# Causal attention with an image token and a tanh recurrence: another beginning and end, image values in column groups, two heads' transposes together

## The reference

```python
q, k, v = split(x @ c_attn_w + c_attn_b)
k_img, v_img = cond @ uk_w.T + uk_b, cond @ uv_w.T + uv_b      # one key, one value a sequence
scores = q @ concat(k_img, k).T / sqrt(32);  scores = where(kj <= qi + 1, scores, -10000)
x = x + (softmax(scores) @ concat(v_img, v)) @ c_proj_w + c_proj_b
xw = x @ Wx + b
h = tanh(h @ Wh + xw[t])  for t in 0..511, h starts as cond;   out = x + h
```

## Time and profile before

| | |
|---|---|
| median of 3 runs | 1640.55 us |
| profiled execution, its span | 1643.75 us, 1642.0 us |
| TensorE busy | 1532.6 us (93%) |
| VectorE, ScalarE, GpSimd busy | 778.3, 665.1, 186.5 us |
| the chain that ended last | PE 86% of the span |
| TensorE's clock in 40 slices | 8 in the second and third, 9 in all others (tenths; 9 is 90% or more) |
| half clock inside the span | about 54 to 67, 81 to 85, 95 to 105 and 1505 to 1511 us, and after the last step |

### The profile page before, as it was taken

How to read it: one execution, slowest core, us unless ns; L and a number is a source line. 1 busy time by engine, 2 the same in 40 slices (tenths; PEclk the granted TensorE clock), 3 DMA queues, 4 the chain that set the end, 5 groups by cost and what they waited for, 6 DMA issues and landing times.

```text
span 1642.0 us, 74143 instructions
## 1 busy us (share of the span) xinstructions
PE 1532.6 (93%) x32749; PEld 1225.9 (75%) x32749; DVE 778.3 (47%) x2687; ACT 665.1 (41%) x2257; POOL 186.5 (11%) x300
## 2 busy tenths in 40 slices
PE   7799999999999999999999999999999999998775
PEld 6677887877777787877878778687787677777554
DVE  4455454445454545545455454554554454554221
ACT  3444444344343434344443443444534444443111
POOL 2111111010110101001010110100101011100000
PEclk9889999999999999999999999999999999999999
DMA  7323122212222223223332232333332332331000
GB/s 231 107 63 82 50 69 66 69 52 71 65 73 75 79 67 92 74 72 88 85 91 77 81 97 75 109 84 84 107 92 72 110 98 82 116 100 28 16 10 15
DMA packets 167903, 130.24 MB, mean 79 GB/s; under 512 B 54264, under 2 KB 153112, under 8 KB 167072
## 3 DMA queue, kind: packets, MB, share of 16 engines
q1 hardware_dynamic: 153792, 92.92, 19.9%
q0 software_dynamic: 13792, 32.58, 7.3%
HBM read 100.00 MB, written 25.43 MB: 76 GB/s over the span
## 4 chain that ended last, share of the span: by engine, by line
PE 86%; DVE 4%; issue 4%; ACT 4%; SPq 1%; DMA 1%; POOL 0%; DVEq 0%; POOLq 0%
PE rec L1056 27%; PE dense L986 10%; PE dense L502 9%; PE dense L504 7%; PE dense L503 7%; PE rec L1047 7%; PE scores L978 5%; PE pv L1003 4%; PE pv L1021 2%; PE scores L1056 2%; DVE pre L882 1%; PE dense L1063 1%; ACT probs L686 1%; ACT states L735 1%; PE dense L1014 1%
## 5 line engine op out<-in xcount | busy, mean ns | idle before, releaser
L1056 PE MATMUL rec<-wh,states 128*32 128x128 f32 x15360 | 516.3, 275 | 19.9 <-ACT states L735 19.2
L1056 PEld LDWEIGHTS rec<-wh,states 128*32 128x32 f32 x15360 | 399.3, 110 | 107.3 <-ACT states L735 46.1
L882 DVE STREAM_TRANSPOSE pre<-rec 128x128 f32<-128x128 f32 x480 | 152.0, 317 | 502.6 <-PE rec L1056 501.2
L735 ACT ACTIVATE states<-pre 128x32 f32<-128x32 f32 x512 | 133.9, 262 | 508.6 <-DVE pre L882 507.6
L686 ACT ACTIVATE probs<-probs,nmax 128x64 f32<-128x64 f32 (+7 forms) x512 | 271.3, 532 | 104.9 <-DVE nmax L826 102.5
L826 DVE CUSTOM_DVE_ANT_0 probs<-scores,msk,nimg 128x64 f32<-128x64 f32 (+7 forms) x512 | 245.2, 502 | 14.6 <-PE scores L978 6.4
L986 PE MATMUL dense<-ident,probs 128*128 128x128 f32 (+1 forms) x1254 | 229.2, 288 | 19.0 <-DVE probsT L836 7.0
L986 PEld LDWEIGHTS dense<-ident,probs 128*128 128x128 f32 (+1 forms) x1254 | 129.2, 135 | 82.1 <-issue 56.7
L502 PE MATMUL dense<-xT_hi,wqkv_hi 128*128 128x256 f32 x488 | 149.6, 307 | 6.7 <-DVE nimg L812 3.5
L836 DVE COPY probsT<-dense 128x256 f32<-128x256 f32 (+4 forms) x240 | 120.2, 501 | 63.3 <-PE dense L986 57.9
L694 ACT COPY probsT<-dense 128x256 f32<-128x256 f32 (+4 forms) x246 | 104.3, 424 | 107.0 <-PE dense L986 106.5
(11 more groups left out here) (138 smaller groups left out, 1766.3 us busy)
## 6 DMA issues: line engine op xcount, KB each, us to landing
vbuf<-v_dram SPq DMA_DIRECT2D x64, 192.0 KB, 2.7
xin<-x SPq DMA_DIRECT2D x64, 128.0 KB, 2.6
v_dram<-vbuf POOLq DMA_DIRECT2D x64, 128.0 KB, 2.8
out<-outs POOLq DMA_DIRECT2D x32, 256.0 KB, 4.2
vbuf<-v_dram SPq DMA_DIRECT2D x64, 128.0 KB, 2.4
kt<-k_dram SPq DMA_DIRECT2D x16, 512.0 KB, 5.6
vbuf<-v_dram SPq DMA_DIRECT2D x32, 256.0 KB, 3.2
k_dram<-knew POOLq DMA_DIRECT2D x60, 128.0 KB, 2.7
```

The costliest lines, as they stand in the source:

```text
L735: act.activation(state_cells(g), pre[:].rearrange("p f (b z) -> p f b z", z=GROUP)[:, :, :, s], ACT.Tanh).then_inc(h_ready, 1)
L882: dve.transpose(pre_all, rec_bank(g // GROUP)[:, 0:P]).then_inc(pre_ready, 1)
L1056: last = pe.matmul(rec_bank(g // GROUP)[Q * j:Q * j + Q, 0:P], state_tile(g - 1)[:, f, :], wh[:, f, P * j:P * j + P], start=False, stop=f ...
```

## The change

1. Beginning. `uk_w` is loaded in two halves, each with its own semaphore. The image key is made with the state as weights (16 matmuls in column groups) and turned on VectorE. `uv_w` is loaded before the second half of `w_qkv`; its transposes come after the first `q` and `k` (`uvturn`). The loads of x for trips 1 and 2, of `w_proj`, and of `w_x` and `w_h` move to units 3, 14, 12 and 20, and the casts of `w_proj` from units 5 to 8 to units 24 to 27.
2. `norm`: the image's values as 16 products of 32 columns instead of 4 of 128.
3. `turn`: at every even u the events of units u - 4 and u - 3 stand together; before, one stood at every u.
4. End. The last two of the 448 steps are laid at the end of their range; the first products of each projection wait for half of the low parts only; the last store is issued by SyncE.

```diff
+        if u == 3:
+            emit([("xload", 1, 0, 0.0)])
...
+        if g == 0 and h in (24, 25, 26, 27):
+            emit([("wproj", 0, h - 24, 0.0)])
...
-        if TURN_LAG <= u < HEADS + TURN_LAG:
-            v = u - TURN_LAG
-            emit([("turn", v, 0, 0.05 + 0.11 * tiles_of(v // UNITS))])
+        if TURN_LAG <= u < HEADS + TURN_LAG and u % 2 == 0:
+
+            emit([("turn", v, 0, 0.05 + 0.11 * tiles_of(v // UNITS)) for v in (u - TURN_LAG, u - TURN_LAG + 1)])
...
         while (t < FIRST and at > ends[(t // W + 1) * QUADS - 1]
+               and (t < FIRST - 2 or at + 1 == last)
                and (done >= max(whole * (t + 0.5) / FIRST, step_at + PACE) or at + 1 == last)):
...
+            if kind == "out" and name == ("POOL" if g == OUTS - 1 else "SP"):
...
+                if kind == "wpload":
+
+                    sp.wait_ge(low_ready, 2 * C)
...
+                    if g == 1:
+
+                        sp.wait_ge(low_ready, C)
...
+                elif kind == "weights":
+
+                    pool.wait_ge(setup_product, 2)
...
-            for c in range(C):
-                for f in range(C):
-                    last = pe.matmul(rec[:, B * c:B * c + B], wx[:, f, P * c:P * c + P], imgT[:, f, :],
-                                     start=f == 0, stop=f == C - 1)
+
+            pe.wait_ge(h_ready, 1)
+            for f in range(C):
+                for j in range(C):
+                    last = pe.matmul(rec[Q * j:Q * j + Q, 0:P], state_tile(-1)[:, f, :],
+                                     wx[:, f, :].rearrange("p (a j c) -> p a j c", a=C, j=C)[:, :, j, :],
+                                     start=f == 0, stop=f == C - 1, skip_group_check=True)
...
                     for c in range(C):
-                        last = pe.matmul(pv[:, P * c:P * c + P], vimg[:, P * c:P * c + P], pimgT[:],
-                                         start=False, stop=True, skip_group_check=True)
+                        for j in range(HC):
+
+                            at = P * c + Q * j
+                            last = pe.matmul(pv[Q * j:Q * j + Q, P * c:P * c + P], vimg[:, at:at + Q], pimgT[:],
+                                             start=False, stop=True, skip_group_check=True)
...
-                    if i == 0:
-                        pe.wait_ge(attn_split, 4 * g + 4)
                     for c in range(C):
+                        if i == 0 and c % 2 == 0:
+
+                            pe.wait_ge(attn_split, 4 * g + 3 + c // 2)
```

More of the change, by code:

```diff
@@ L67 @@
     "ACT": {"xsplit": 0.0, "q": 0.2, "softmax": 0.8, "turn": 0.2, "imgprob": 0.2, "imgturn": 0.2,
-            "rowturn": 0.2, "norm": 0.6, "step": 0.5, "out": 0.2, "wproj": 0.0},
-    "POOL": {"mskload": 0.9, "mskscale": 1.0, "vstore": 1.0, "out": 1.0, "k": 0.7, "vimg": 1.6},
-    "SP": {"xload": 0.8, "vimgload": 0.9, "k": 0.7, "kqload": 0.8, "vload": 0.5},
+            "rowturn": 0.2, "norm": 0.6, "step": 0.5, "out": 0.2, "wproj": 0.0, "uvturn": 0.2},
+    "POOL": {"mskload": 0.9, "mskscale": 1.0, "vstore": 1.0, "out": 1.0, "k": 0.7, "vimg": 1.6,
+             "weights": 0.0},
+    "SP": {"wpload": 0.0, "xload": 0.8, "vimgload": 0.9, "k": 0.7, "kqload": 0.8, "vload": 0.5, "out": 1.0},
 }
@@ L157, in main_order @@
             side, until = (chunk(g, 3) + values(g, 0) if g == 0 else []) + values(g, 1), 9 if g else 5
-        if g == 0 and h in (5, 6, 7, 8):
-            emit([("wproj", 0, h - 5, 0.0)])
+        if u == 3:
+            emit([("xload", 1, 0, 0.0)])
+        if u == 12:
+            emit([("wpload", 0, 0, 0.0)])
+        if u == 14:
+            emit([("xload", 2, 0, 0.0)])
+        if u == 20:
+            emit([("weights", 0, 0, 0.0)])
+        if g == 0 and h in (24, 25, 26, 27):
+            emit([("wproj", 0, h - 24, 0.0)])
         if u == 9:
@@ L403, in attention_recurrence @@
         image_ready = sem("image_ready")
+        image_turned = sem("image_turned")
+        uk_loaded = [sem(f"uk_loaded{k}") for k in range(2)]
         kimg_ready = sem("kimg_ready")
@@ L542, in _ @@
         def _(sp):
-            for tile, a in ((ident[:], ident_in), (cond_sb, cond), (uk_raw, uk_w)):
+            for tile, a in ((ident[:], ident_in), (cond_sb, cond)):
                 sp.dma_start(tile, a).then_inc(key_loaded, 16)
+            for k in range(2):
+                half = slice(D // 2 * k, D // 2 * (k + 1))
+                sp.dma_start(uk_raw[:, :, half], uk_w[:, :, half]).then_inc(uk_loaded[k], 16)
             for n, i in enumerate(SPLITS):
@@ L579, in _ @@
                                  .rearrange("b p t -> p b t")).then_inc(tile_loaded[g % LOADS], 16)
+                elif kind == "out":
+                    wait_copied(sp, kind, g, 0)
+                    sp.dma_start(out[:, g * HALF:(g + 1) * HALF, :], outs[:]).then_inc(last_stored, 16)
                 elif kind == "vload":
@@ L676, in _ @@
                     act.copy(in_pairs(xT_hi[:, 2 * i:2 * i + 2, :]), x_halves(g, i)).then_inc(xT_high, 1)
+                elif kind == "uvturn":
+                    for f, d in enumerate(scores):
+                        act.wait_ge(setup_turned, C + 2 + f)
+                        act.copy(wh[:, f, :], d[:, :]).then_inc(values_copied, 1)
                 elif kind == "q":
@@ L899, in _ @@
             for f, d in enumerate(scores):
+                if f % 2 == 0:
+                    pe.wait_ge(uk_loaded[f // 2], 16)
                 for o in range(C):
@@ L903, in _ @@
             pe.wait_ge(setup_copied, 1 + C)
-            for c in range(C):
-                for f in range(C):
-                    last = pe.matmul(rec[:, B * c:B * c + B], wx[:, f, P * c:P * c + P], imgT[:, f, :],
-                                     start=f == 0, stop=f == C - 1)
-            last.then_inc(setup_product, 1)
-            pe.wait_ge(value_loaded, 16)
-            for f, d in enumerate(scores):
-                for o in range(C):
-                    last = pe.transpose(d[:, P * o:P * o + P], uv_raw[:, o, P * f:P * f + P], ident[:])
-                last.then_inc(setup_turned, 1)
+            pe.wait_ge(h_ready, 1)
[4 more added lines that the diff above has]
+                                     start=f == 0, stop=f == C - 1, skip_group_check=True)
+            last.then_inc(setup_product, 1)
             for kind, g, i in ORDER["PE"]:
@@ L941, in _ @@
                         last.then_inc(dense_ready, 1)
+                elif kind == "uvturn":
+                    pe.wait_ge(value_loaded, 16)
+                    for f, d in enumerate(scores):
+                        for o in range(C):
+                            last = pe.transpose(d[:, P * o:P * o + P], uv_raw[:, o, P * f:P * f + P], ident[:])
+                        last.then_inc(setup_turned, 1)
                 elif kind == "vimg":
```

23 lines of the change are left out of this document (13 added, 10 removed).

## The result

The changed kernel takes 1653.09 us, the median of 5 runs (1652.66 to 1655.89). The kernel before took 1641.07 beside it. The ratio is 1.0069, interval 1.0054 to 1.0085: slower by 9 to 14 us. Forecast was 1636.5 in a range of 1627 to 1648, so sign and range were both missed. The profiled execution took 1652.96 us, its span 1651.1.

What follows compares the result with a forecast made beforehand. TensorE, busy 93% of the span, was taken as the bound. Start and round trip -1.5, short trips +2, image values -4.5, changes of form -12.5, banks +16, end -2.5 and -1.0 sum to -4.0: 1640.55 to 1636.5 us, range 1627 to 1648.

Steps and rivals of the forecast that it cites:

- The start: Before the loop: image values start at 26.9 us instead of 29.94, 3.0 saved, at most 1.5 lost to half clock.
- The first round trip: First wait for values: first product with v near 52 us; with the start only -1.5 us, as x loads come late.
- Image values: 32-column products in groups replace wide ones in 32 blocks, less added changes of form: -4.5 us, bound 0.
- The banks, same bank: Pairs where the values hold a bank: the second set waits for the first's copy, 11 pairs at 1.0 us, +11.
- The banks, other pairs: The other 245 pairs: the second set may wait for the other bank's copy, 0.02 us each, +5, bounds 0 and +25.
- Changes of form: TensorE switching to transposes and back: 57 fewer such pairs of changes at 0.22 us, -12.5, bounds -16 and -6.
- Short trips: First trips (64 and 128 keys): the odd head's softmax has less time, so TensorE waits: +2 us, bounds 0 and +8.
- that rival: The clock falls: longer transpose runs drop TensorE's clock in late trips, +30 us, 1666; chance 0.06.
- Banks dominate: Rival at the second set of a pair: bank waits make the kernel slower, 1646 to some 1656; chance 0.19.
- The sign named for the forecast: Waits of transposes for VectorE's and ScalarE's copies rise by some 16 us if the forecast is right.
- A steady stretch that is not shorter: Sign that the forecast is wrong: the span from step 0 to step 447 does not shrink.
- The end: Last trip: held-back steps fill the wait -1.2, projection's clock -1.3, last store from SyncE -1.0 us.

Runs made afterwards that it cites:

- begin_only: The kernel before with the changed beginning alone: 1637.3 us, ratio 0.9973.
- norm_only: The kernel before with the image values in column groups alone: 1637.8 us, ratio 0.9965.
- split_same: The changed kernel with the 13 pairs whose two sets share one bank issued one head per unit: 1642.4 us, ratio 1.0001 to before.
- single: The changed kernel with one head's transposes at every unit instead of pairs: 1632.7 us, ratio 0.9937 to before.
- onebank: The changed kernel with both heads of a pair in one bank, copied by one instruction, in trips one to eight: 1615.1 us, ratio 0.9828 to before.
- pairs_first_two: The changed kernel with pairs in the first two trips alone, one head per unit elsewhere: 1642.3 us, ratio 1.0002 to before.
- end_only: The kernel before with the changed end alone: 1640.9 us, ratio 0.9988.
- onebank_two_copies: Like onebank, but each pair is copied by two instructions and its bank freed after the second: 1617.8 us, ratio 0.9858 to before.

## Why the prediction was wrong

In short: the parts without the pairs brought -10.3 us where -9.5 was forecast (-1.5, -4.5, -2.5, -1.0). The pairs cost 21.7 where some +6 was forecast (+2, -12, +16). So the step that failed is the price of the pairs. Term by term:

**The start** was right: image values at 27.20 (26.9 forecast), first product with v at 52.37 (52). I had taken that L946 might fall to half clock; it ran at full clock.

**The first round trip** was too low: head 8's transposes came 4.4 us early instead of 1.5. The values' loads were issued from 48.2 us on instead of 49.7, SyncE's loads of x by 53 instead of 54.6, and ScalarE began its last cast of x at 55.2, where I had the last landing at 57.5. `begin_only` has -4.4 to before.

**Image values:** -4.5 forecast, -5.7 measured (interval -7.9 to -3.4). Right, with some luck. From start to the transposes behind it is 1.00 us (299.56 to 300.56), 1.09 before, and not the 0.90 that I had named as its sign: over 32 blocks that is 2.9 us. `norm_only`'s runs lose 3.0 us less to the clock than the kernel before beside them (18.0 against 21.0, taken as above), and I had not counted on that. My sum was also a little off: 1.09 less 0.90 is 0.19, and 32 of those less 1.2 are -4.9.

**The banks, same bank,** +11 forecast: "That is so in 11 pairs", 1.0 us each. There are 13, and they cost 11 to 12 us together. Right.

**The banks, other pairs,** +5 forecast, are the first half of the step that failed: "In the other 245 pairs ... I take 0.02 a pair, +5". In the stretch from the third trip on, `split_same`, which has only such pairs (211 there), takes 1349.2 us without its half-clock stretches and `single` 1346.8. So these pairs lose 2.4 us after all that they save. Taken with the saving of the next item (8 to 11 us) they cost 10 to 13 us, 0.05 to 0.06 a pair. I had asked only what stands in front of a pair (a step hides that copy) and not what stands behind it. A pair fills both banks, and the dense chunk, the image scores or the next transposes behind it wait for the first copy. The rows show it: dense products wait 7.8 us for VectorE's copies where with singles they wait 1.9. It is dearest where a trip is short, in trips three and four (7.3 us in 32 pairs, net, one of them in the same bank); I had one price for all trips.

**Changes of form,** -12 forecast for the pairs. In the order, `single` has 550 pairs of changes, after 496, so the pairs do save 54, 11.9 us at the 0.22 of the prediction. No run shows that apart. `onebank`, with the same 496, has TensorE busy 8.1 us less than `single` from the third trip on; the changed kernel only 2.0 less. The 6 us between may be waits too short to show as idle time, which is argued and not shown. So this term was 4 us too high, or more.

**Short trips,** +2 forecast, are the other half of the failed step. As a softmax that comes late the term was right: 20.5 to 23.7 us in the waits, and `onebank` has the same deadlines and loses nothing. But the pairs cost 7 to 11 us in the first two trips (21.7 less 14.8, and `pairs_first_two`), 5 to 7 of them through a lower clock, for which the prediction had no term. I had looked for the clock's fall only in long runs of transposes from 160 us on, where it hardly fell (1.00 over the whole stretch). Why it was lower in the first trips stays open. The rule of the Trainium skill behind that rival (TensorE: Matmul & The Clock Gate, Part 4: PE-mode transpose) finds no support here: the runs of transposes in `onebank` are as long as those after, and its runs lose least to the clock of all kernels (11.3 us on average).

**The rivals and the signs.** "Banks dominate" gave 1656 with 0.1 us a pair. The time is close and the direction right, but partly by luck: the pairs cost about half of that, and the clock in the first trips made up for it. The sign named for the forecast, waits for the copies up by some 16 us, nearly came (14.3 to 33.3), and "over 25 us more" did not; so this sign could not tell a faster kernel from a slower one. A steady stretch that is not shorter is the sign that told.

**The end:** -1.2 for the steps, -1.3 for the clock and -1.0 for the store were forecast; `end_only` has -2.0 (-4.1 to +0.2). From the last image values to the projection the time is 4.38 us with two steps in it, where there was one in 4.3, so some 0.9 was won. The projection to step 448 takes 7.9 instead of 10.6 us at full clock, but that stretch is one of those that come and go: `split_same` and `pairs_first_two` have the new end and a half-clock stretch there. The store's term is 0.45 (8.29 less 7.84): the Trainium skill (DMA: Bandwidth & Descriptors, Specifications) gave 0.4, nearer than my 1.0 from the landing times.

Part of the pairs' price depends on the rest: +14.6 on the old beginning, +21.7 on the new. From the third trip on it is nearly the same (12.8 and 14.8 us), so most of the difference lies in the first two trips. There the clock goes with it: the pairs raise its loss by 6.8 us on the new beginning (16.3 to 23.1) and by 1.7 on the old (21.8 to 23.5). The intervals of the two prices (10.7 to 18.7, and some 17 to 26) overlap a little.

## What to carry to other kernels

When several kinds of work rotate through two PSUM banks, price a reordering by bank places: put two users back to back only if they can share one bank and one release, and look at what stands behind them as much as at what stands in front. Where TensorE has gaps already, expect an order to move the clock too: here that was 5 to 7 us in two short trips, and compare it over several executions, since one trace can mislead by as much. And less busy time in a window of fixed length (here 13.1 us) can be plain idle time: compare the same work from its first to its last instruction.

## What was not expected of the hardware

- Two copies of half the width took longer than one. The copies in `onebank`, and then in `onebank_two_copies` (line, engine, work, count, busy us, mean ns of one, idle before):

```profile
L499 DVE COPY probsT<-dense 128x512 f32<-128x512 f32 (+2 forms) x56 | 32.0, 572 | 11.8 <-PE dense L1049 11.2
L499 ACT COPY probsT<-dense 128x512 f32<-128x512 f32 (+2 forms) x57 | 27.6, 484 | 15.5 <-PE dense L1049 15.2
```

```profile
L499 DVE COPY probsT<-dense 128x256 f32<-128x256 f32 (+2 forms) x56 | 20.3, 362 | 12.0 <-PE dense L1049 11.5
L500 DVE COPY probsT<-dense 128x256 f32<-128x256 f32 (+2 forms) x56 | 19.9, 355 | 0.0
...
L499 ACT COPY probsT<-dense 128x256 f32<-128x256 f32 (+2 forms) x57 | 18.1, 317 | 15.9 <-PE dense L1049 15.7
```

  On VectorE it is 572 ns against 362 + 355 (means over the same three shapes): the second instruction costs 145 ns of its own.
- Sixteen transposes of `uv_w` took 3.58 us at the start before and 1.91 in their new place, 0.12 us each, directly behind products with no idle time between. The difference is the clock. The record of the kernel before has no entry before 26.6 us, but `end_only`, with the same beginning, shows it at half there, and the same transposes take 3.67 us:

```profile
15.00:28.60 13.60, 7.15 (x35) 7.05 (x36) 6.94 (x13) 6.60 (x10) 3.45 (x8) 0.50 0.75 272
```

```profile
23.41 3.67 PE L921 MATMUL scores<-ident,vbuf 128*128 128x128 f32 x16 [6.45 <-DMA vbuf<-uv_w]
```

  So the prediction's guess, "as if at half clock", was right.
- Half-clock stretches came and went late in the program, in the same order of instructions: `pairs_first_two` had one at 1066 us, `single` none, 1.7 us each.
